# Softmax attention on one core: row maxima read from two adjacent PSUM banks at once, probabilities computed one head at a time in single banks

## What is computed

```python
q, k, v = (qkv[0], qkv[1], qkv[2])
scores = jnp.einsum('bhqd,bhkd->bhqk', q, k) / np.sqrt(HD).astype(np.float32)
causal = jnp.triu(jnp.ones((s, s), dtype=bool), 1)
scores = jnp.where(causal[None, None], -jnp.inf, scores)   # first attention only
attn_w = jax.nn.softmax(scores, axis=-1)
attn = jnp.einsum('bhqk,bhkd->bhqd', attn_w, v)
```

## Time and profile before

| | |
|---|---|
| median of 3 runs | 4475.92 us (4475.87 to 4476.56) |
| span of the profiled execution, first to last instruction | 4472.3 us |
| its own time | not listed beside the span; the median is 3.6 us above it |
| busy: TensorE, VectorE, ScalarE, GpSimd | 75%, 64%, 41%, 25% of the span |
| exponentials, L2025 | 896, 794.5 us |
| row maxima, L2051 and L2048 | 1280 in 800.7 us, 512 in 230.4 us |
| first-pass scores, L1971 | 1792 matmuls |
| mean granted TensorE clock over the span | 0.851 |

### The profile page before, as it was taken

The page is one execution under the profiler, slowest core; times in us unless marked ns, Lnnn a source line. Parts: engine busy times, 40 slices in busy tenths (PEclk is TensorE's granted clock), DMA queues, the critical chain, the costliest instruction groups (busy, mean ns, idle before and its releaser), DMA issues. The chain is left out here.

```text
span 4472.3 us, 64693 instructions
## 1 busy us (share of the span) xinstructions
PE 3373.7 (75%) x19639; PEld 2051.6 (46%) x19639; DVE 2863.6 (64%) x6999; ACT 1834.9 (41%) x2613; POOL 1133.7 (25%) x1292
## 2 busy tenths in 40 slices
PE   3547999866554496799999936957957695997798
PEld 2422333323333385222222225846946585886587
DVE  6857888676685444899999654445555555554553
ACT  1123666633211153277777812522411232562364
POOL 2420000044344543100000055436610654000100
PEclk8766999977776698599999967978976798998899
DMA  8912101000000212200000022121210122000000
GB/s 120 98 43 52 31 26 32 3 0 0 19 0 23 68 48 73 75 16 21 19 24 17 2 77 87 49 70 47 63 46 29 35 60 68 1 0 1 1 0 19
DMA packets 178667, 163.52 MB, mean 37 GB/s; under 512 B 26640, under 2 KB 152144, under 8 KB 177488
## 3 DMA queue, kind: packets, MB, share of 16 engines
q1 hardware_dynamic: 160528, 123.49, 12.4%
q0 software_dynamic: 17280, 35.69, 2.4%
q10 hardware_dynamic: 576, 0.79, 0.1%
HBM read 88.33 MB, written 70.75 MB: 36 GB/s over the span
## 5 line engine op out<-in xcount | busy, mean ns | idle before, releaser
L2025 ACT ACTIVATE core_pr<-core_two 128x1024 f32<-128x1024 f32 (+3 forms) x896 | 794.5, 933 | 441.6 <-PE core_two L1987 440.7
L2051 DVE TENSOR_REDUCE core_mx<-core_one 128x1 f32<-128x512 f32 x1280 | 800.7, 682 | 22.9 <-PE core_one L1971 19.5
L1971 PE MATMUL core_one<-arena,core_q_sb 64*128 64x512 bf16 (+3 forms) x1792 | 548.6, 381 | 105.5 <-DMA core_q_sb<-core_q_sb 42.9
L1971 PEld LDWEIGHTS core_one<-arena,core_q_sb 64*128 64x128 bf16 x1792 | 140.3, 94 | 689.4 <-DVE core_mx L2051 525.7
L1998 PE MATMUL core_ps_o<-core_pr,core_vals 128*32 128x512 f32 (+3 forms) x3584 | 438.6, 561 | 1.6 <-ACT core_oT L2029 0.5
L1987 PE MATMUL core_two<-core_q_sb,arena 64*128 64x512 bf16 (+3 forms) x1792 | 362.1, 361 | 6.4 <-ACT core_pr L2025 5.4
L1946 POOL COPY core_vals<-arena 128x288 f32<-128x288 f32 x32 | 14.4, 453 | 1131.6 <-PE core_ps_o L1998 1131.4
L2048 DVE CUSTOM_DVE_ANT_0 core_junk<-core_one,behind 128x128 bf16<-128x128 f32 (+3 forms) x512 | 230.4, 486 | 59.6 <-PE core_one L1971 54.3
L377 POOL DMA_INDIRECT expert_out<-arena,moe_first_desti x142 | 144.0, 1014 | 172.4 <-ACT arena L583 147.3
L377 POOL DMA_INDIRECT expert_out<-arena,moe_second_desti x142 | 144.0, 1014 | 172.1 <-ACT arena L583 145.3
L502 PE MATMUL moe_first_bank<-arena 128*128 x1136 | 150.4, 275 | 1.5 <-ACT arena L583 1.5
(11 more groups left out here) (541 smaller groups left out, 7782.2 us busy)
## 6 DMA issues: line engine op xcount, KB each, us to landing
expert_rows<-zero SPq DMA_DIRECT2D x1, 19175.0 KB, 150.9
arena<-expert_rows SPq DMA_DIRECT2D x284, 65.0 KB, 1.8
arena<-expert_out SPq DMA_DIRECT2D x64, 256.0 KB, 4.1
core_q_sb<-q_parts SPq DMA_DIRECT2D x384, 32.0 KB
arena<-k_parts SPq DMA_DIRECT2D x360, 32.0 KB
arena<-in_m_up SPq DMA_DIRECT2D x16, 512.0 KB, 4.0
q_parts<-qkv_parts SPq DMA_DIRECT2D x16, 384.0 KB, 2.6
k_parts<-qkv_parts SPq DMA_DIRECT2D x16, 384.0 KB, 3.1
```

What stands on the lines that cost most here:

```text
L1971: pe.matmul(one[bank][:, 0:width], q_sb[rows, hq, pair, qt * P:(qt + 1) * P], k_sb[rows, hq, pair, kc * CW:kc * CW + width], start=True, s ...
L2025: a.activation(pr[:, k % 2, hp, :, off:CW], two[hp][:, :, off:CW], ACT.Exp, scale=HD ** -0.5).then_inc(s_exp, 1)
L2051: v.tensor_reduce(mx[:, h * TPB + qt, kc:kc + 1], one[bank][:, 0:width], AX.X, ALU.max).then_inc(s_read, 1)
```

## The change

The eight banks are dealt out anew: `one` becomes two buffers of two adjacent banks (1024 columns), `two` three single banks, `ps_o` stays. A read covers all keys of a query tile, so there are 32 per group in either stage; the fold `rows` falls away, and `mx` is double-buffered by group. In core0 every read goes through the masked instruction, against a mask tile of 1024 columns. In the second pass, each head has its own matmul, wait, bank and exponential (128x512); bank u % 3 is free when the exponential three turns before it is done. The planner's loop has a slot behind each head's scores, starts its second pass one step ahead instead of two, and puts `out` right behind a weigh.

```diff
-    one = [st.ps(f"one{i}") for i in range(3)]
-    two = [st.ps(f"two{i}", (P, 2, CW)) for i in range(2)]
+    one = [st.ps(f"one{i}", (P, SEQ)) for i in range(2)]
+    two = [st.ps(f"two{i}") for i in range(3)]
...
-            keys = (qt + 1) * P if causal else SEQ
-            for kc in range(-(-keys // CW)):
-                width = min(CW, keys - kc * CW)
-                for side in range(2):
-                    tiles.append((2 * pair + side, qt, kc, width, causal and (kc + 1) * CW >= keys))
+            for side in range(2):
+                tiles.append((2 * pair + side, qt, (qt + 1) * P if causal else SEQ))
...
-                fill += [("rows", 0, ahead), None, None, ("maxima", 0, ahead)]
+                fill += [None, None, ("maxima", 0, ahead)]
...
-        for k in range(2, N2 + 2):
-            for hp in range(2):
+        for k in range(1, N2 + 1):
+            for h in range(GH):
                 if k < N2 or more:
-                    events.append((f"second{hp}", k % N2, k // N2))
+                    events.append((f"second{h}", k % N2, k // N2))
                 slot()
-            if k <= N2 or more:
-                events.append(("weigh", (k - 1) % N2, (k - 1) // N2))
+            events.append(("weigh", k - 1, 0))
+            if moved is not None:
+                events.append(("out", moved, 0))
+                moved = None
             if k - 1 in ends:
                 moved = ends.index(k - 1)
                 events.append(("move", moved, 0))
-                slot(), slot()
-            else:
-                slot()
-                if moved is not None:
-                    events.append(("out", moved, 0))
-                    moved = None
-                slot()
+        events.append(("out", moved, 0))
...
+                    for at in range(0, width, CW):
+                        cut = slice(at, min(at + CW, width))
+                        mm = pe.matmul(one[bank][:, cut], q_sb[rows, hq, pair, qt * P:(qt + 1) * P], k_sb[rows, hq, pair, cut],
+                                       start=True, stop=True)
+                    mm.then_inc(s_first, 1)
...
+                    u = turn(n, k, h)
...
+                    if u >= 3:
+                        pe.wait_ge(s_exp, u - 2)
                     if mask:
-                        for i in range(2):
-                            pe.matmul(two[hp][:, i, off:off + P], g.identb[:], g.mask_k, start=True, stop=False, skip_group_check=True)
+                        pe.matmul(two[u % 3][:, off:off + P], g.identb[:], g.mask_k, start=True, stop=False, skip_group_check=True)
+                    rows, pair = lane(h)
+                    pe.matmul(two[u % 3][:, off:CW], k_sb[rows, hq, pair, j * P:(j + 1) * P], q_sb[rows, hq, pair, c * CW + off:(c + 1) * CW],
+                              start=not mask, stop=True, skip_group_check=mask).then_inc(s_second, 1)
...
-                    a.activation(pr[:, k % 2, hp, :, off:CW], two[hp][:, :, off:CW], ACT.Exp, scale=HD ** -0.5).then_inc(s_exp, 1)
+                    a.activation(pr[:, k % 2, h // 2, h % 2, off:CW], two[u % 3][:, off:CW], ACT.Exp, scale=HD ** -0.5).then_inc(s_exp, 1)
...
-                    if mask:
-                        v.tensor_tensor_reduce(junk[:, bank, 0:width], one[bank][:, 0:width], g.behind[:, CW - width:CW], 1.0, -3.0e38,
-                                               ALU.add, ALU.max, mx[:, h * TPB + qt, kc:kc + 1]).then_inc(s_read, 1)
+                    if causal:
+                        v.tensor_tensor_reduce(junk[:, bank, 0:width], one[bank][:, 0:width], g.behind[:, SEQ - width:SEQ], 1.0, -3.0e38,
+                                               ALU.add, ALU.max, top).then_inc(s_read, 1)
                     else:
-                        v.tensor_reduce(mx[:, h * TPB + qt, kc:kc + 1], one[bank][:, 0:width], AX.X, ALU.max).then_inc(s_read, 1)
+                        v.tensor_reduce(top, one[bank][:], AX.X, ALU.max).then_inc(s_read, 1)
...
-        g.behind = sb("behind", [P, CW])
+        g.behind = sb("behind", [P, SEQ])
```

More of the change, by code:

```diff
@@ L1819, in plan @@
             if ks[-1] == N1 - 1:
-                fill += [("rows", 0, ahead), None, None, ("maxima", 0, ahead)]
+                fill += [None, None, ("maxima", 0, ahead)]
         if not second:
-            return [e for e in fill if e] + [(f"second{hp}", k, more) for k in range(2) for hp in range(2)] + [("weigh", 0, more)]
+            return [e for e in fill if e] + [(f"second{h}", 0, more) for h in range(GH)]
         slots, events = 4 * N2, []
@@ L1867, in over_groups, with turn @@
             group(BATCH - 1, hq, [(1, tail), (2, head)][:min(left, 2)], steady if left else [("maxima", 0, 0), ("out", 1, -1)], True, min(left, 1))
[L1875 to L1878, removed]
+    (s_first, s_read, s_neg, s_mst, s_mld, s_second, s_exp, s_weighed, s_moved, s_turned, s_normed, s_rec, s_vals,
+     s_zero, s_ones) = (
+        st.sem(n) for n in ("first", "first_read", "neg", "m_stored", "m_loaded", "second", "exp", "weighed", "moved",
+                            "turned", "normed", "recip", "vals", "zero", "ones"))
     s_loaded = [st.sem(f"loaded{i}") for i in range(GROUPS)]
     LOADS = 16 * 2 * (2 * len(PAIRS) + 1)
+    def turn(n, k, h):
+        return (n * N2 + k) * GH + h
     def lane(h):
@@ L1953, in _ @@
         def _(pe):
-            pe.sem_inc(s_second, 8 * N2)
+            pe.sem_inc(s_second, 4 * GH * N2)
             pe.sem_inc(s_weighed, 2 * N2)
@@ L1970, in emit @@
                         pe.wait_ge(s_loaded[hq], (b + 1) * LOADS)
-                    pe.matmul(one[bank][:, 0:width], q_sb[rows, hq, pair, qt * P:(qt + 1) * P],
-                              k_sb[rows, hq, pair, kc * CW:kc * CW + width], start=True, stop=True).then_inc(s_first, 1)
+                    for at in range(0, width, CW):
+                        cut = slice(at, min(at + CW, width))
+                        mm = pe.matmul(one[bank][:, cut], q_sb[rows, hq, pair, qt * P:(qt + 1) * P], k_sb[rows, hq, pair, cut],
+                                       start=True, stop=True)
@@ L1973, in emit @@
+                    mm.then_inc(s_first, 1)
                 elif what == "maxima":
-                    pe.wait_ge(s_row, n + 1)
-                    pe.matmul(one[bank][0:GH * TPB, 0:P], mrow[:], g.ident[:], start=True, stop=True).then_inc(s_first, 2)
-                elif what in ("second0", "second1"):
+                    pe.wait_ge(s_read, n * (N1 + 2) + N1 + 2)
+                    pe.matmul(one[bank][0:GH * TPB, 0:P], mx[:, n % 2, :], g.ident[:], start=True, stop=True).then_inc(s_first, 2)
+                elif what.startswith("second"):
@@ L1985, in emit @@
-                    for i in range(2):
-                        rows, pair = lane(hp * 2 + i)
-                        mm = pe.matmul(two[hp][:, i, off:CW], k_sb[rows, hq, pair, j * P:(j + 1) * P],
-                                       q_sb[rows, hq, pair, c * CW + off:(c + 1) * CW], start=not mask, stop=True, skip_group_check=mask)
-                    mm.then_inc(s_second, 1)
+                        pe.matmul(two[u % 3][:, off:off + P], g.identb[:], g.mask_k, start=True, stop=False, skip_group_check=True)
@@ L2067, in emit @@
                     v.wait_ge(s_turned, 2 * n + k + 3)
-                    heads = one[bank][:].rearrange("p (t h m) -> p t h m", t=CT, m=32)
+                    heads = one[bank][:, 0:CW].rearrange("p (t h m) -> p t h m", t=CT, m=32)
                     v.reciprocal(rec[:, k], heads[:, :, :, HD]).then_inc(s_rec, 1)
@@ L2491, in _ @@
                 sp.dma_start(g.mask_f[:], d["mask"][:, 1]).then_inc(s_first, 16)
-                sp.dma_start(g.behind[:, CW - P:CW], d["mask"][:, 0]).then_inc(s_first, 16)
+                sp.dma_start(g.behind[:, SEQ - P:SEQ], d["mask"][:, 0]).then_inc(s_first, 16)
                 sp.dma_start(g.routes.table[:], d["route"]).then_inc(s_first, 16)
@@ L2502, in _ @@
                 v.memset(g.inv_e[:], float(np.exp(-1.0))).then_inc(s_set, 1)
-                v.memset(g.behind[:, 0:CW - P], 0.0).then_inc(s_set, 1)
+                v.memset(g.behind[:, 0:SEQ - P], 0.0).then_inc(s_set, 1)
                 v.wait_ge(s_first, 96)
```

36 lines of the change are left out of this document (16 added, 20 removed).

## The result

The changed kernel takes **5098.17 us** (median of 4 runs, 5087.13 to 5116.95), the kernel before in the same session 4476.24 (4475.87 to 4479.43): ratio 1.1398, 95% interval 1.1381 to 1.1415. It is slower, as forecast, but by 622 us where 358 were forecast, and outside the range of 4750 to 4900. The profiled execution has a span of 5085.3 us against 4472.3.

What follows compares the result with a forecast made beforehand. VectorE was taken to bound core1 and TensorE core0. Core1 +235, core0 +125 and small terms -2 made 358 us on a span of 4472.3; with 3.6 up to the median, 4834 us, range 4750 to 4900.

Steps and rivals of the forecast that it cites:

- the crowding: Planner puts core1's reads in the first nine of 16 iterations, seven have none; core0 crowded too, 1.6 us more.
- clock at 1.00 in both: Sign expected in the changed kernel's profile: TensorE's granted clock at 1.00, or 2.4 GHz, in core0 and core1.
- the clock falls: Rival: core1's full iterations drop to 1.2 GHz, 7.1 us each instead of 4.6, 280 us at worst; total 4974; chance 0.08.
- Order of events, core1: Reads first, then iterations without reads: core1's group takes 58.6 us, 15.4 more; whole stage +235 us.
- bare iterations: Core1 iterations without reads, set by a ring of three banks for four heads: seven a group, 2.40 us each.
- full ones: Core1 iterations with four 1024-column reads: 4.52 us on VectorE, more than TensorE's 3.7.
- the out: Last out of a group stands right behind the last weigh, so TensorE waits 0.80 us for ScalarE's copy, both stages.
- reads: One 1024-column read on VectorE takes 1.13 us, against 1.20 for two of 512; 2.1 us gained per core1 group.
- Core0: TensorE-bound stage, summed at 28.9 of 30.5 us a group before; period becomes 38.4, 7.9 more; +125 us in all.
- masks: Core0 mask matmuls, now one per head: 8.6 us a group instead of 5.1.
- unpaired matmuls: Core0 second-pass matmuls, each alone between reads: 7.7 us a group instead of 3.8.
- About half: The share of the 280 us worst case in core1 expected if the clock goes up and down, giving 4974 us.

Runs made afterwards that it cites:

- filler: The change plus useless TensorE work in core1: 16 extra 512-column matmuls a group; ratio 1.1342 to the kernel before.
- even and later: The change with reads spread evenly over the group and each group's last out moved behind the next group's first weigh; ratio 1.0459 to the kernel before.
- half the masks: The change with even reads and later last out, without core0's mask matmuls of heads 1 and 3; ratio 1.0306 to the kernel before.
- out later: The change with only each group's last out moved behind the first weigh of the next group; ratio 1.1095 to the kernel before.
- filler and later: The change with 16 useless matmuls a group in core1 and each group's last out moved later in both stages; ratio 1.0931 to the kernel before.

## Why the prediction was wrong

The direction, the mechanism of the crowding and nearly all sizes held. **The step that failed is "clock at 1.00 in both"**: the forecast priced every matmul at 2.4 GHz and gave the rival "the clock falls" 0.08. That rival is what happened.

- *Order of events, core1:* right, 57.87 against 57.8 where the clock is held up. Its parts too: bare iterations 2.39 (2.40); full ones at 1.00 4.59 us apart with and without filler (4.52), and with filler most of a group's first ones 4.80 (4.79); the out 0.80; reads 1.143 (1.13).
- *Core0:* 38.4 was forecast. At 1.00 even and later gave 35.9, where the forecast's terms without out and crowding make 38.4 - 0.8 - 1.6 = 36.0. That it met is luck: masks were 3.0 for 3.5 and unpaired matmuls about 2.4 for 3.9, 2.0 too much together, and the sum started from 28.9 and not from the 30.5 of before, 1.6 too little. What the crowding and the out would cost core0 at 1.00 was not measured by itself.
- *Rival 2, "the clock falls":* its full iteration at the low clock, 7.1 us, was 6.74. A mean clock of 0.82 means that 0.36 of the period is at the low level: 0.36 x 66.61 = 24 us, or 3.6 iterations of 6.74. At 2.14 us more than at full clock each that is 7.7 us, and the period exceeds the forecast by 8.0. "About half" for core1 was then near: 112 us measured, 140 forecast. The rival left core0 out altogether, and core0 lost as much again (132 us), so its 4974 is also 124 us too low.
- *Why it got 0.08:* the evidence against it was a row that did not bear on the case. Core1's end without reads the earlier trace rows is all bare iterations, and those stand at 1.00 after the change as well. The nearest row to a crowded iteration was core1's opening, TensorE feeding reads, at 0.50. The forecast had itself worked out that full iterations go at VectorE's pace, in core1, and that the out adds a wait at each group's end in both stages. It weighed the clock for the first in a rival alone, and for the second, and for core0, not at all.
- *Range:* its terms were added at one clock, so none of its ends reached the other level.

The Trainium skill's page "TensorE: Matmul & The Clock Gate" names the pattern in its section "A second HAM failure mode: psum-queue depth-cycling": a TensorE that idles briefly and often between groups of matmuls, because of a ring of PSUM banks, goes back and forth between the two clocks. Core1 here agrees in kind: in each of the twelve groups the clock stands at 1.00 in the bare iterations and is at 0.50 in a part of the crowded ones, about a third of the period. Its way of pricing it, half of the throttled time (section "Terms"), would be an estimate of 0.36 x 66.61 / 2 = 12.0 us a group in core1 for a mean clock of 0.82, where the period exceeds the forecast by 8.0. That reads and exponentials cover the rest is likely, since TensorE still waits for reads at the low clock, but no run shows it by itself.

**Shown:** crowding alone brings the clock down in the banks and pairs of before; even reads bring it back in core1; in core1 the low clock is worth 7.6 us a group, with more work, and the order at full clock 12.6; the out's place matters for core0, and for core1 once filler is there. In core0 out, crowding and lost pairs each have a part: 0.71 became 0.86, 0.83 and 0.85 with one of them undone, 0.91 with the first two, 0.97 with all three. **Open:** what sets off the falls that are left in single groups of core0, and why unpaired matmuls bring it down while TensorE hardly waits. The next group's transfers stand at the same place in core0 (DMA share 0.30 to 0.33 where it falls); no run moved them, and filler was not tried there.

## What to carry to other kernels

When a change makes one stretch of a loop wait and another not, price it at both levels of the TensorE clock and give both a real chance. An old profile at 1.00 may owe that to evenly spread work, as it did here. A greedy "ceil(items / slots left)" is even only while items outnumber slots: halve the items, and they crowd into the front half. To settle whether the clock is what costs, give TensorE useless work in a place that another engine's time hides. Here the kernel became faster by it.

## What the runs showed of the hardware that was not expected

- TensorE's busy share in a slice does not tell its clock. In the even and later run, core0, three-us slices around a dip:

```profile
481.80:484.80 3.00, 2.55 (x20) 1.05 (x19) 2.68 (x7) 2.12 (x5) 0.46 (x1) 1.00 0.30 92
484.80:487.80 3.00, 3.00 (x16) 1.15 (x15) 0.40 (x4) 0.92 (x2) 0.00 (x0) 0.64 0.32 100
487.80:490.80 3.00, 3.00 (x21) 0.96 (x19) 1.99 (x8) 1.53 (x4) 0.00 (x0) 0.79 0.10 32
```

  It falls where TensorE is busy 3.00 of 3 us, behind a slice of 2.55, while bare iterations of core1 stand at 1.00 with 3.05 of 4. What core0 issues there are single second-pass matmuls on half of the array and masks of 128 columns; with the matmuls in pairs the dip is gone in nine of twelve groups, and with half of the masks alone left out it is not (half the masks: 0.95 in its usual group, too).
- Groups of equal work alternate between two states, 59.2 and 70.3 us, strictly in turn (the filler run, core1): here the clock's falls keep step with the groups.
- Sixteen matmuls more a group made core1 7.6 us a group faster (out later alone, against filler and later, on another chip).
